# A routed expert stage with stationary weights, blocks of 448 tokens, and pad rows written during attention

## The chip, the cores and the metric

The kernel runs on one core of one Trainium2 chip. The metric is the device time of one execution in microseconds; the figure for the kernel before is the median of three runs. A difference of 0.3% (1.6 us) is about what such a measurement can tell from no change.

## The reference

Sixteen sequences of 100 tokens, 256 wide, go through a local cross-attention (16 heads, window 64) and then a feed-forward layer of eight experts with two experts per token. All in fp32. Cut to what matters here:

```
x = x + attention(layernorm(x), ctx)                 # 1600 tokens
xf = layernorm(x)
topk_p, topk_i = top_k(softmax(xf @ router_w.T), 2)
for e in range(8):
    mask   = (topk_i == e).any(-1)                   # tokens of expert e
    mean_w = mean of the normalised weights of those tokens
    h      = silu(xf @ gate_w[e].T) * (xf @ up_w[e].T)   # 256 -> 1024
    out   += mask * (h @ down_w[e].T) * mean_w           # 1024 -> 256
x = x + out
```

With the reference's own inputs the router gives the eight experts 374, 410, 299, 390, 438, 418, 425 and 446 tokens, 3200 in all. In tiles of 128 these are 3, 4, 3, 4, 4, 4, 4 and 4 tiles, 30 in all, as many as the trace has; in blocks of 448 they are one block each.

## The kernel before

**Attention stage.** Eight pairs of sequences go through a software pipeline written out in the code, one iteration of eight steps per pair. For each pair SP sends 16 small transfers (`kblk<-krot`, line 361) that spread the rotated keys over block-diagonal tiles; the scores (line 421) of the pair read them, so that SP's queue holds, in order, the key blocks of the next pair, then the store of the finished pair. Meanwhile the normalised rows and the row number of each token are scattered by POOL (line 1186) into a DRAM buffer `slots`, which has a region for each expert. ACT's queue loads the weights of expert 0 (`w_raw`, 3 MB) in iteration 1, and POOL splits them into a high and a low part.

**Between the stages.** DVE counts the tokens of each expert and makes a plan of tiles. POOL scatters a row of zeros behind the last token of each expert (`tailrow`, line 1223, eight scatters), so that the last tile of each expert is filled. SP waits for the scatters (line 385), reads the plan into registers, waits for the pad rows of the expert and loads a tile of 128 rows (`xin`, line 394).

**Expert stage.** Every fp32 product is made of three fp32r products: high x high, high x low, low x high. For a tile of 128 tokens TensorE keeps the tokens stationary: `x_hi` or `x_lo` (128 x 128) is loaded and 512 columns of the gate or up weights move (lines 615 to 617; 24 matmuls per tile, in two halves of the hidden width). The result has tokens on the partitions; ACT takes the silu, DVE multiplies (`h_sb`, line 1097), and TensorE transposes h in eight 128 x 128 pieces (line 631) into two banks, from which ACT makes `h_hi` (line 780) and DVE `h_lo` (line 1102). The down product (line 640) has h stationary and 256 columns of the down weights moving, 24 matmuls per tile. DVE copies the 128 x 256 result out (line 1109), POOL scales it by the mean weight (line 1245) and adds it to the output rows with an indirect transfer (line 1250).

**What sets the order.** Each engine has its own program, a loop over tiles inside a loop over experts; semaphores tie them. The gate and up of the next tile's first half (`hidden(next_par, 0)`) stand between the two halves of the down product, so that TensorE has work while h is prepared. The weights of the next expert are loaded a whole expert ahead into one of two buffers `w_raw`, and ACT (line 787) and DVE (line 1116) split them in 12 pieces of 512 columns, four in each of three tiles.

## Time and profile before

| | |
|---|---|
| three runs | 530.47, 531.59, 532.20 us; median 531.59 |
| span of the profiled execution | 528.9 us |
| TensorE matmuls busy | 476.4 us, 90% |
| TensorE weight loads busy | 375.3 us, 71% |
| DVE, ACT, POOL busy | 321.5, 265.6, 186.4 us |
| data moved | 46.26 MB, 87 GB/s in the mean |

The profiled execution is 2.7 us shorter than the median of the runs; sums below are made in its time and carried over by adding this. The page also has, for each of 40 slices of 13.2 us, the granted TensorE clock: full in nearly all, lower in slice 16 and 17, where the program passes from attention to the experts. The stages are: attention until about 200 us, routing and the first tile until 225 us, 30 tiles until 516 us, and a tail.

### The profile page before, as it was taken

The page shows a single profiled execution, that of the slowest core. Times are in us where ns is not written, and L with a number is a line of the kernel's source. Part 1 is how long each engine was busy: PE and PEld are TensorE (multiplying, and loading weights), DVE is VectorE, ACT ScalarE, POOL GpSimd, SP SyncE. Part 2 cuts the span into 40 slices and gives each one's busy share as a digit, 9 for nine tenths or more (in the row PEclk, how much of TensorE's full clock was granted, in tenths as well). Part 3 has the DMA queues.
Part 4 walks back from the last instruction along what each step waited for, and adds up shares of the span by engine and source line. Part 5 has one row for each costly group of instructions (what it writes and reads, how often), then busy time and mean ns, then how long its engine had stood idle before and what let it go on. Part 6 is the DMA issues. An engine that isn't in the chain of part 4 may idle for free. (4 is left out here: it accounts for less than half of the span.)

```text
span 528.9 us, 10721 instructions
## 1 busy us (share of the span) xinstructions
PE 476.4 (90%) x2879; PEld 375.3 (71%) x2880; DVE 321.5 (61%) x827; ACT 265.6 (50%) x878; POOL 186.4 (35%) x211
## 2 busy tenths in 40 slices
PE   2999999999999983199999999999999999999980
PEld 2656666665666542078888888888888888888870
DVE  3476988989998656345665456655655555553430
ACT  1287777677777870044544445544444444532320
POOL 5201327355372434712332323323333232232232
PEclk9699999999999995579999999999999999999996
DMA  7166102112020171371531634415317212112110
GB/s 210 33 184 241 32 12 54 32 34 63 7 58 14 50 286 47 96 274 32 168 117 35 215 83 139 147 32 196 101 20 256 42 20 32 27 21 39 20 20 10
DMA packets 21738, 46.26 MB, mean 87 GB/s; under 512 B 5032, under 2 KB 18600, under 8 KB 20684
## 3 DMA queue, kind: packets, MB, share of 16 engines
q10 hardware_dynamic: 1982, 23.29, 11.6%
q1 hardware_dynamic: 12974, 14.34, 9.3%
q0 software_dynamic: 6752, 8.29, 9.2%
q8 instruction: 11, 0.18, 0.1%
q14 instruction: 19, 0.16, 0.1%
HBM read 34.21 MB, written 10.04 MB: 84 GB/s over the span
## 5 line engine op out<-in xcount | busy, mean ns | idle before, releaser
L752 ACT ACTIVATE probs<-b_s,negmax 100x100 f32<-100x100 f32 x256 | 85.6, 358 | 25.2 <-DVE negmax L1005 21.8
L615 PE MATMUL b_s<-w_hi,x_hi 128*128 128x512 f32 x180 | 77.1, 428 | 1.1 <-issue 1.1
L617 PE MATMUL b_s<-w_hi,x_lo 128*128 128x512 f32 x180 | 72.3, 402 | 0.0
L616 PE MATMUL b_s<-w_lo,x_hi 128*128 128x512 f32 x180 | 72.2, 401 | 0.0
L640 PE MATMUL b_pv<-w_hi,h_hi 128*128 128x256 f32 x240 | 69.8, 291 | 1.4 <-DVE h_lo L1102 1.4
L640 PE MATMUL b_pv<-w_hi,h_lo 128*128 128x256 f32 x240 | 67.4, 281 | 0.0
L640 PE MATMUL b_pv<-w_lo,h_hi 128*128 128x256 f32 x240 | 67.3, 280 | 0.0
L1245 POOL TENSOR_SCALAR y_sb<-y_raw,mean 128x256 f32<-128x256 f32 x30 | 32.8, 1093 | 75.9 <-DVE y_raw L1109 75.7
L1250 POOL DMA_INDIRECT out<-y_sb,idnow x30 | 49.1, 1638 | 25.6 <-issue 23.0
L780 ACT CAST h_hi<-b_small 128x512 fp32r<-128x512 f32 x30 | 17.6, 587 | 80.7 <-PE b_small L631 80.7
L1116 DVE TENSOR_TENSOR w_lo<-w_raw,w_hi x84 | 57.3, 682 | 0.0
L752 ACT ACTIVATION_READ_ACCUMULATOR probs<-b_s,negmax 100x1 f32 x256 | 55.9, 218 | 0.0
L421 PE MATMUL b_s<-kblk,qrot 128*100 128x400 f32 x128 | 54.3, 505 | 0.0
L1102 DVE TENSOR_TENSOR h_lo<-b_small,h_hi 128x512 fp32r<-128x512 f32 x30 | 20.8, 692 | 55.0 <-ACT h_hi L780 55.0
L787 ACT CAST w_hi<-w_raw x84 | 52.2, 621 | 0.0
L776 ACT ACTIVATE act<-b_s 128x512 f32<-128x512 f32 x60 | 36.0, 600 | 28.6 <-PE b_s L617 28.6
L640 PEld LDWEIGHTS b_pv<-w_hi,h_hi 128*128 128x128 f32 x240 | 45.2, 188 | 3.0 <-DVE h_lo L1102 1.6
L640 PEld LDWEIGHTS b_pv<-w_lo,h_hi 128*128 128x128 f32 x240 | 45.3, 189 | 1.4
L640 PEld LDWEIGHTS b_pv<-w_hi,h_lo 128*128 128x128 f32 x240 | 45.2, 188 | 0.0
L1005 DVE TENSOR_REDUCE negmax<-b_s 100x4 f32<-100x400 f32 x64 | 36.2, 565 | 14.8 <-PE b_s L421 14.2
L1097 DVE TENSOR_TENSOR h_sb<-b_s,act 128x512 f32<-128x512 f32 x30 | 20.8, 692 | 34.7 <-PE b_s L617 34.7
L1176 POOL TENSOR_SCALAR ve<-mv 100x2 f32<-100x2 f32 x16 | 3.6, 228 | 103.8 <-DVE mv L859 103.8
(142 smaller groups left out, 1004.1 us busy)
## 6 DMA issues: line engine op xcount, KB each, us to landing
w_raw<-in_ffw ACTq DMA_DIRECT2D x7, 3072.0 KB, 10.1
xin<-slots SPq DMA_DIRECT2D x30, 128.5 KB
w_raw<-in_ffw SPq DMA_DIRECT2D x1, 3072.0 KB, 10.8
kblk<-krot SPq DMA_DIRECT2D x128, 12.5 KB, 1.8
out<-x_all SPq DMA_DIRECT2D x8, 200.0 KB
ctx_all<-in_ctxT SPq DMA_DIRECT2D x1, 1200.0 KB, 6.1
x_all<-in_x SPq DMA_DIRECT2D x1, 1200.0 KB
cst<-in_consts SPq DMA_DIRECT2D x1, 539.0 KB, 7.5
```

The source lines that it names most:

```text
L421: pe.matmul(o, qrot[:, i % 2, 2 * c + b, :], kblk[:, i % 2, c, h:h + QH, b * S:(b + 1) * S], start=False, stop=True).then_inc(s_s, 1)
L615: pe.matmul(o, lh, rh, start=(k == 0), stop=False)
L616: pe.matmul(o, lh, rl, start=False, stop=False)
L617: m = pe.matmul(o, ll, rh, start=False, stop=(k == n - 1))
L640: m = pe.matmul(b_y[:, 0:D], left[:, f, :], right[:, f, :], start=(f == 0 and k == 0), stop=(f == FC - 1 and k == 2))
L752: m = nc.scalar.activation(probs[:, N % 3, h, :], b_s[N % 3][0:S, h * S:(h + 1) * S], ACT.Exp, bias=negmax[:, N % 4, h:h + 1], accum_out=p ...
L776: nc.scalar.activation(act[:, half, :], b_gate[half][:, :], ACT.Silu).then_inc(s_act, 1)
L787: nc.scalar.copy(w_hi[1 - par][:, bass.ds(col, WC)], w_raw[par][:, bass.ds(col, WC)]).then_inc(s_whi, 1)
L1005: V.tensor_reduce(negmax[:, N % 4, :], b_s[N % 3][0:S, 0:QH * S].rearrange("p (h s) -> p h s", h=QH), AX.X, ALU.max, negate=True).then_inc ...
L1116: V.tensor_tensor(w_lo[1 - par][:, bass.ds(col, WC)], w_raw[par][:, bass.ds(col, WC)], w_hi[1 - par][:, bass.ds(col, WC)], ALU.subtract).t ...
L1245: G.tensor_scalar(y_sb[:, :], y_raw[:, :], mean1[:, 0:1], None, ALU.mult).then_inc(s_scaled, 1)
L1250: G.indirect_dma_start(out, bass.IndirectOffsetOnAxis(idnow[:, 0:1], 0), y_sb[:, :], None, bounds_check=TOK + P - 1, oob_is_err=True, comp ...
```

## The change

The expert stage is written anew, and the pad rows are written elsewhere.

- **Blocks.** A tile is now 448 tokens in four groups of 112 rows. `xin` is loaded as 112 partitions of four rows and transposed in 2 x 4 pieces of 112 columns into two banks.
- **Gate and up.** The weights are stationary (128 x 128) and 448 token columns move: 12 matmuls for each of eight strips f of 128 hidden features. The result has features on the partitions, which the down product wants, so h isn't transposed; `h_sb` is split by ACT and DVE from SBUF instead of PSUM.
- **Down.** For each strip and group, h (128 x 112) is stationary and 256 columns move, 12 matmuls per strip; the four groups' results lie in two banks. Strip f's down product stands behind the gate and up of strip f+2. The gate and up of the next block's strip 0 stand ahead of this block's last down strip.
- **Transpose of the next block** stands ahead of strip 7; its evacuation (`x_high` on ACT, `x_low` on DVE) can only begin when strip 7 has read the old `x_hi`.
- **Output.** ACT copies the two banks out with the mean weight as scale; POOL only issues four indirect transfers per block.
- **Weights.** One `w_raw` buffer, loaded, split and reloaded in six pieces of 1024 columns, one in each of strips 0 to 5 of an expert's first block.
- **Pad rows.** A host array `padrows` (448 rows of zeros with row numbers past the end) is copied by SP over the whole of `slots`, from DRAM to DRAM, in attention iterations 0 to 3: eight transfers of 461 KB in each, behind the key blocks of the next pair. POOL's scatter waits for those that cover its rows. The eight scatters of `tailrow` are gone, and so is SP's wait for them. The spare rows of the output are filled from `padrows` too (459 KB instead of 131 KB).

The diff, cut to its core:

```diff
-            sp.wait_ge(s_zero, 2)
-            sp.dma_start(out[TOK:TOK + P, :], tailrow[:, 0:D]).then_inc(s_pad, 16)
+            sp.dma_start(out[TOK:TOK + TILE, :], padrows[:, 0:D]).then_inc(s_pad, 16)
...
+            def fill_pads(j):
+                for e in range(E):
+                    base = e * REGION + j * TILE
+                    sp.dma_start(slots[base:base + TILE, :].rearrange("(p g) w -> p (g w)", g=GRP),
+                                 padrows.rearrange("(p g) w -> p (g w)", g=GRP)).then_inc(s_pre[j], 16)
...
             for i in pairs:
                 if i + 1 < NPAIR:
                     key_blocks(i + 1)
+                if i < MAXT:
+                    fill_pads(i)
                 if i >= 1:
                     store_x2(i - 1)
...
+            def hidden(par, f):
+                cols = slice(f * P, (f + 1) * P)
                 for which, banks, done in ((0, b_gate, s_gate), (1, b_up, s_up)):
                     wh, wl = wpart(w_hi[par])[which], wpart(w_lo[par])[which]
+                    o = banks[f % 2][:, 0:TILE]
+                    for c in range(DC):
+                        pe.matmul(o, wh[:, c, cols], x_hi[:, c, :], start=(c == 0), stop=False)
+                        pe.matmul(o, wh[:, c, cols], x_lo[:, c, :], start=False, stop=False)
+                        m = pe.matmul(o, wl[:, c, cols], x_hi[:, c, :], start=False, stop=(c == DC - 1))
...
-            def hidden_transpose(t, half):
-                pe.wait_ge(s_h, 2 * t + half + 1)
-                for f in range(HF):
-                    m = pe.transpose(b_ht[half][:, f * TILE:(f + 1) * TILE],
-                                     h_sb[:, half, f * P:(f + 1) * P], ident)
...
+            def step(t, par, next_par, next_split, following):
+                for f in range(1, FC):
+                    if f >= 2:
+                        pe.wait_ge(s_h, FC * t + f - 1)
+                    if f == FC - 1:
+                            pe.wait_ge(s_xlo, t + 1)
+                            tile_transpose(t + 1)
+                    hidden(par, f)
+                    if f >= 2:
+                        project_down(par, t, f - 2)
+                project_down(par, t, FC - 2)
+                    pe.wait_ge(s_wlo, next_split)
+                    pe.wait_ge(s_xlo, t + 2)
+                    hidden(next_par, 0)
+                project_down(par, t, FC - 1)
...
+            def take_output(t, e):
+                a.wait_ge(s_down, t + 1)
+                for n in range(GRP // 2):
+                    m = nc.scalar.activation(y_sb[:, 2 * n:2 * n + 2, :].rearrange("p g d -> p (g d)"),
+                                             b_y[n][0:ROWS, :], ACT.Copy, scale=meanw[0:ROWS, e:e + 1])
...
+                for n in range(GRP):
+                    G.indirect_dma_start(out, bass.IndirectOffsetOnAxis(idnow[:, n:n + 1], 0), y_sb[:, n, :], None,
```

How the order changes, at three places.

TensorE, from the last matmuls of a down half to the gate and up of the next tile, of the kernel before (`h_hi`, `h_lo` stationary; `x_hi` stationary; the wait `s_xlo` is for the next tile's tokens):

```order
L640 MATMUL b_pv<-w_lo,h_hi 128x256
L640 MATMUL b_pv<-w_hi,h_lo 128x256
L629 REGISTER_ALU
L631 MATMUL b_o<-cst,h_sb 128x128 [waits s_h]
L631 MATMUL b_o<-cst,h_sb 128x128 x3
L615 MATMUL b_s<-w_hi,x_hi 128x512 [waits s_xlo,s_wlo]
L616 MATMUL b_s<-w_lo,x_hi 128x512
L617 MATMUL b_s<-w_hi,x_lo 128x512
```

The same place of the kernel after, between two blocks:

```order
L628 MATMUL b_small<-w_lo,h_hi 112x256
L628 MATMUL b_small<-w_hi,h_lo 112x256
L615 MATMUL b_s<-x_hi,w_hi 128x448 [waits s_xlo,s_wlo]
L616 MATMUL b_s<-x_lo,w_hi 128x448
L617 MATMUL b_s<-x_hi,w_lo 128x448
```

The transposes of h are gone; the wait for the next tokens stands right behind a down strip, and what lies between strip 7's last gate and up matmul and this wait is two down strips, 24 matmuls.

SP's queue in the first iterations of attention, before (`kblk` are the key blocks of one pair, 16 transfers):

```order
L361 DMA kblk<-krot 16x200 [waits s_krot]
L361 DMA kblk<-krot 16x200 x15
L361 DMA kblk<-krot 16x200 [waits s_s,s_krot]
L361 DMA kblk<-krot 16x200 x15
L367 DMA out<-x_all 100x2x256 [waits s_x2]
```

and after:

```order
L345 DMA kblk<-krot 16x200 [waits s_krot]
L345 DMA kblk<-krot 16x200 x15
L357 DMA slots<-in_padrows 16x7196 x8
L345 DMA kblk<-krot 16x200 [waits s_s,s_krot]
L345 DMA kblk<-krot 16x200 x15
L357 DMA slots<-in_padrows 16x7196 x8
L351 DMA out<-x_all 100x2x256 [waits s_x2]
```

Eight copies of pad rows, of 16 pieces of 28.8 KB each, stand ahead of the key blocks of pair 2, and again ahead of those of pairs 3, 4 and 5.

ACT in a strip of an expert's first block, after:

```order
L771 ACTIVATE act<-b_s 128x448 [waits s_gate]
L775 CAST h_hi<-h_sb 128x448 [waits s_h]
L780 CAST w_hi<-w_raw 128x1024 [waits s_raw1_]
L784 DMA w_raw<-in_ffw 128x1024 [waits s_wlo]
L770 REGISTER_ALU
L771 ACTIVATE act<-b_s 128x448 [waits s_gate]
```

where before it had, in a tile with weight pieces:

```order
L780 CAST h_hi<-b_small 128x512 [waits s_ht]
L787 ISA
L787 COPY w_hi<-w_raw 128x512
L775 REGISTER_ALU
L776 ACTIVATE act<-b_s 128x512 [waits s_gate]
```

ACT now also waits, in each strip, for a piece of weights from DRAM and for DVE's split of the piece before.

## Rows read from the trace of the kernel before

**Rows 1.** The page, part 1: busy us (share of span) and instructions by engine.
```profile
PE 476.4 (90%) x2879; PEld 375.3 (71%) x2880; DVE 321.5 (61%) x827; ACT 265.6 (50%) x878; POOL 186.4 (35%) x211
```

**Rows 2.** Three stretches: us, busy us (xinstructions) by engine, granted clock, DMA.
```profile
core 0: us, PE busy (x) PEld busy (x) DVE busy (x) ACT busy (x) POOL busy (x), PEclk, DMA share, GB/s
0.00:218.00 218.00, 186.52 (x1139) 121.28 (x1140) 165.78 (x532) 138.57 (x643) 89.62 (x106) 0.94 0.27 84
218.00:231.00 13.00, 6.16 (x15) 4.18 (x15) 1.18 (x3) 2.25 (x3) 7.19 (x9) 0.51 0.45 128
231.00:516.00 285.00, 283.60 (x1726) 249.89 (x1726) 154.08 (x291) 124.83 (x232) 86.89 (x93) 1.00 0.33 92
```

**Rows 3.** Timeline of TensorE in one steady tile: start us, us, line, operation.
```profile
302.75 0.60 PE L631 MATMUL b_o<-cst,h_sb 128*128 128x128 f32 x4
303.10 0.48 PE L615 MATMUL b_s<-w_hi,x_hi 128*128 128x512 f32 x1
303.42 0.40 PE L616 MATMUL b_s<-w_lo,x_hi 128*128 128x512 f32 x1
303.66 0.39 PE L617 MATMUL b_s<-w_hi,x_lo 128*128 128x512 f32 x1
...
305.99 0.28 PE L640 MATMUL b_pv<-w_hi,h_hi 128*128 128x256 f32 x1
...
307.41 0.60 PE L631 MATMUL b_small<-cst,h_sb 128*128 128x128 f32 x4
```

**Rows 4.** Groups by shape, 250 to 500 us: busy us, mean ns | idle before.
```profile
L1116 DVE TENSOR_TENSOR w_lo<-w_raw,w_hi x76 | 51.8, 682 | 0.0
L787 ACT CAST w_hi<-w_raw x76 | 47.2, 621 | 0.0
L1102 DVE TENSOR_TENSOR h_lo<-b_small,h_hi 128x512 fp32r<-128x512 f32 x27 | 18.7, 692 | 49.3 <-ACT h_hi L780 49.3
L780 ACT CAST h_hi<-b_small 128x512 fp32r<-128x512 f32 x27 | 15.8, 587 | 71.9 <-PE b_small L631 71.9
L1087 DVE TENSOR_TENSOR x_lo<-b_proj,x_hi 128x256 fp32r<-128x256 f32 x26 | 10.9, 420 | 0.0
L772 ACT CAST x_hi<-b_proj 128x256 fp32r<-128x256 f32 x26 | 9.7, 374 | 16.8 <-PE b_proj L608 16.8
```

**Rows 5.** The one wait of SP on line 385, for the last scatter into slots.
```profile
L385 SPq EVENT_SEMAPHORE  x1: 28/28/28, 218.0 to 218.0; - x1
```

**Rows 6.** Timeline of all engines where the expert stage begins.
```profile
221.20 27.13 SPq L394 DMA_DIRECT2D xin<-slots  x4
222.91 0.66 PE L608 MATMUL b_proj<-cst,xin 128*128 128x128 f32 x2 [6.27 <-DMA xin<-slots]
223.66 0.37 ACT L772 CAST x_hi<-b_proj 128x256 fp32r<-128x256 f32 x1 [12.26 <-PE b_proj L608]
...
224.71 0.77 PE L615 MATMUL b_s<-w_hi,x_hi 128*128 128x512 f32 x1 [1.14 <-issue]
```

**Rows 7.** Timeline of all engines in the tail.
```profile
515.79 0.28 PE L640 MATMUL b_pv<-w_hi,h_lo 128*128 128x256 f32 x1
...
518.55 1.60 POOL L1250 DMA_INDIRECT out<-y_sb,idnow  x1 [0.84 <-issue]
```

**Rows 8.** The last wait of the program, on line 399, for the last added rows.
```profile
L399 SPq EVENT_SEMAPHORE  x1: 28/28/28, 522.5 to 522.5; - x1
```

**Rows 9.** Queues, 40 to 60 us, ACT queue: packets, MB, share of 16 engines.
```profile
q10 hardware_dynamic: 144, 3.15, 39.9%
```

**Rows 10.** Timelines of SP and PE: key blocks 2 and 3 sent, then read.
```profile
50.76 1.61 SPq L361 DMA_DIRECT2D kblk<-krot  x2
...
60.34 0.84 PE L421 MATMUL b_s<-kblk,qrot 128*100 128x400 f32 x2
...
71.75 10.31 SPq L361 DMA_DIRECT2D kblk<-krot  x16
...
82.79 0.84 PE L421 MATMUL b_s<-kblk,qrot 128*100 128x400 f32 x2
```

More of the change, by code:

```diff
@@ L61 @@
 C_BASE = C_EXP + E
[L62 to L63 removed]
+C_THR = C_BASE + E
 C_LT = C_THR + E * (MAXT - 1)
@@ L637, in project_down @@
+                    m.then_inc(done, 1)
+            def project_down(par, t, f):
+                pe.wait_ge(s_hlo, FC * t + f + 1)
+                if f == 0:
+                    pe.wait_ge(s_y, t + 1)
                 wh, wl = wpart(w_hi[par])[2], wpart(w_lo[par])[2]
-                for f in range(half * HF, (half + 1) * HF):
+                for g in range(GRP):
+                    o = b_y[g // 2][0:ROWS, g % 2 * D:(g % 2 + 1) * D]
                     for k, (left, right) in enumerate(((h_hi, wh), (h_hi, wl), (h_lo, wh))):
-                        m = pe.matmul(b_y[:, 0:D], left[:, f, :], right[:, f, :],
-                                      start=(f == 0 and k == 0), stop=(f == FC - 1 and k == 2))
@@ new lines, in step @@
+            def step(t, e, par, split, again, final=False):
+                for f in range(FC):
+                    if f:
+                        if f == FC - 1 and not final:
+                            a.wait_ge(s_up, FC * (t + 1))
+                            x_high(t + 1)
+                        silu(t, f)
+                    hidden_high(t, f)
+                    if split and f < WCH:
+                        weights_high(e, par, f)
+                    if split and again and 1 <= f <= WCH:
+                        reload(e, f - 1)
@@ new lines, in step @@
+            def step(t, e, par, split, final=False):
+                for f in range(FC):
+                    if f:
+                        if f == FC - 1 and not final:
+                            x_low(t + 1)
+                        gated(t, f)
+                    hidden_low(t, f)
+                    if split and f < WCH:
+                        weights_low(e, par, f)
+                    if f == FC - 2 and not final:
+                        v.wait_ge(s_idnow, t + 1)
+                        take_ids(t + 1)
```

396 lines of the change are left out of this document (151 added, 245 removed).

## The prediction, made before the changed kernel was run

> **What bounds the kernel now.** I read the busy time of the engines first: TensorE has matmuls in flight for 476.4 of 528.9 us [rows 1]. The table by stretch then says where: in the expert loop, 231 to 516 us, it is busy 283.6 of 285 us at the full clock, 2.4 GHz, while DVE, ACT and POOL are at half or less [rows 2]. So the stage is worth what TensorE's list of instructions costs, and nothing else. In attention (0 to 218 us) TensorE shows 186.5, DVE 165.8 and ACT 138.6 us: a chain through several engines. The change leaves its arithmetic alone, but puts 14.7 MB of copies under it. Between the stages TensorE runs at a mean granted clock of 0.51, that is at its lower level of 1.2 GHz, until 231 us [rows 2].
>
> **Gate, up and down.** The starts in one steady tile give the price of a matmul [rows 3]: from the second gate matmul (303.42) to the first down matmul (305.99) there are 11 of 512 columns, 0.2336 us each; from there to 307.41 are 12 of 256 columns, 0.1183 each. Both weight loads hide behind them. The line through the two gives 0.2048 us for 448 columns. A block has 96 of 448 and 96 of 256 columns: 19.66 + 11.36 = 31.02 us, eight blocks 248.2 us. The same work before was 30 tiles of 24 x 0.2336 + 24 x 0.1183 = 8.45 us, 253.4 us. So less padding (3584 rows instead of 3840) brings only 5 us; most is in what follows.
>
> **Transposes.** Before, each tile has two groups of four pieces of h. Four take 0.35 us (302.75 to 303.10), and the first matmul behind them is 0.32 instead of 0.234 us, so 0.435 a group, 0.87 us a tile, 26.1 us in 30 tiles; all of it goes. The transposes of x were two per tile and are eight per block: at 0.0875 each, with one transition of 0.085, 0.78 us a block, seven of them inside the loop, 5.5 us.
>
> **The seam between blocks.** `x_hi` has one buffer, so the next tokens can be evacuated only after strip 7's last gate and up matmul has started, at T. It shows 0.39 us [rows 3]; ACT starts 0.09 us after PE's end at stage entry (222.91 + 0.66 to 223.66) [rows 6]. ACT's casts cost 374 ns at 256 and 587 at 512 columns, DVE's subtractions 420 and 692 [rows 4]: at 448 columns 534 and 624, two of each now. The two hand-overs in this chain were 1.05 - 0.37 - 0.42 = 0.26 us (of the time from 223.66 to 224.71) [rows 4, 6]. Sum: T + 0.39 + 0.09 + 1.07 + 1.25 + 0.26 = T + 3.06. TensorE has two down strips to do meanwhile, until T + 0.205 + 24 x 0.1183 = T + 3.04. So the cover is just used up. I take 0.2 us for each of seven seams, 1.4 us, with bounds of 0 and 1 us each. Strip 7's own h (multiply, cast, subtract) is hidden by the 2.46 us of the next block's strip 0.
>
> **ACT and DVE per strip.** The weights are split in pieces of 1024 columns: at the same slopes a cast of 621 ns at 512 becomes 1.05 us, a subtraction of 682 ns 1.23 us [rows 4]. Cast of h, cast of weights, subtraction, next multiply form a ring: 0.57 + 1.05 + 1.23 + 0.62 + about 0.2 = 3.7 us, against TensorE's 2.46 + 1.42 = 3.88 per strip. It fits, and h has more than a strip of slack; two full 512-wide prices instead (1.24, 1.36) would make it 4.0 and cost some 0.1 x 6 x 7 = 5 us, less that slack. I take 0.
>
> **First hidden to last down matmul.** Before 515.79 - 224.71 = 291.1 us [rows 6, 7]. After 248.2 + 5.5 + 1.4 + the low clock. Before, it lasted about 6.3 us from the first matmul to 231 us [rows 2]; at half the rate this loses 3.1 us, and I take the same. Together 258.2: **-32.9 us**.
>
> **Stage entry.** The last scatter has landed at 218.0 [rows 5] and SP issues `xin` at 221.20 [rows 6]; in these 3.2 us SP loads two registers, now done ahead of the wait, and computes the address, still behind it. The gain lies between 0 and 3.2; I take half, -1.6. The load took 1.7 us for 131 KB; the 332 KB more cost 0.87 us at the rate below. Six more transposes at 1.2 GHz cost 6 x 0.175 = 1.05; x_high grows from 0.37 to 1.07, x_low from 0.42 to 1.25. Sum **+1.85 us**. The eight `tailrow` scatters on POOL lay beside all this and give nothing beyond the wait.
>
> **Tail.** Before, from the last matmul's start to the last indirect transfer's start 2.76 us, 3.95 to the end of the last wait, 6.4 to the end of the span [rows 7, 8]. After: 0.37, two ACT copies of 512 columns at 0.59 [rows 4], 0.84 until POOL starts [rows 7], then three more transfers at 1.60 and a gap of some 0.3 before the last: 8.1 us. **+5.3 us** (4 to 6, by how much 112 rows save on 128).
>
> **Pad rows during attention.** No row shows a copy from DRAM to DRAM. The nearest is the weight load: 3.15 MB took 39.9% of 16 engines over 20 us, 8.0 us of all of them, 394 GB/s [rows 9]; that is the upper end. A copy has DRAM at both its ends, and I take half, 197 GB/s, as the value, since nothing shows read and write sharing this path for free. A fill of eight copies is 3.69 MB: 9.4 or 18.7 us. The first goes out right behind key blocks 1, at about 40.5 us, and shares the engines with expert 0's weight load from 43.6. Key blocks 2 follow on the same queue from 50.8, and the scores want the first half at 60.3 [rows 10]. At full rate 3.69 + 3.15 MB are through by 59: no delay. At half rate, each engine taking a 28.8 KB piece in 2.3 us in turn with the load's 21.9 KB in 0.9, the fill is done at about 67 and the scores are 7 us late. I take **+6 us**, bounds 0 and 7.7. The later fills are alone: the second starts at about 62, is done by 82 to 87, and blocks 3 are wanted at 82.8 + 6 [rows 10]: just covered, and so the next two. The issues themselves (8 per fill) lie in SP's idle time, 62 to 71.75. POOL waits for the fills only an iteration or more later. The 459 KB copy at the start meets a DMA that is busy with the first loads: +0 to 1.5, I take **+0.5**.
>
> The Trainium skill gives a measured rate for this. "DMA: Bandwidth & Descriptors", section "Latency and other measured facts", has copies between two DRAM tensors at 207 to 214 GB/s in each direction. By it a fill takes 17.2 us and the first delay is about 5 us instead of 6; no run of before shows it.
>
> **Sum.** 528.9 - 32.9 + 1.85 + 5.3 + 6 + 0.5 = 509.65 us; the profiled execution is 2.66 below the median, so **512.3 us**.
>
> **Rivals.**
> 1. *The fills cost nothing.* If DRAM to DRAM runs near 394 GB/s, the 6 us go: 506.3. For: the DMA engines' share is only 0.27 in attention [rows 2]. Against: every byte goes through DRAM twice.
> 2. *Seams cost more.* At each block's end ACT must be free at T, SP's tokens there, and TensorE's program jumps over a loop body three times as long as before, behind 12 queued down matmuls that cover 1.42 us. If the chain or a fetch of code costs 0.6 to 1.9 us at each of eight seams, that is 5 to 15 us: 517 to 527. Against: before, the loops of 30 tiles jump as often and only 1.4 of 285 us are without matmul [rows 2]. The Trainium skill, "Runtime: NRT & Kernel Launch", section "Instruction fetch mechanics", says a taken branch to a place outside the pages at hand stalls until the target is fetched; no row of before shows such a stall in this loop.
> 3. *Slower than before.* The fills run so slowly that all four hold back the key blocks of the pair behind them. Between the start of a fill and the need of those blocks lie some 20 us. At rate r a fill takes 3690/r us (r in GB/s) and each of the last three costs what exceeds 20, the first 8 more. The loss reaches the 25 us that decide at a fill of about 24 us, 150 GB/s; at 120 GB/s a fill takes 31 us, 3 x 11 + 19 = 52 us: 558. Against: that is under two fifths of what the weight load shows [rows 9].
> 4. *More gained.* Fills free and entry, tail and low clock at their lower ends: 500 to 503.5.
>
> **Chances.** Forecast (509 to 516) 0.42; fills free, 505 to 508, 0.24; dearer seams, 517 to 527, 0.15; slow fills 0.11, of which 0.08 end slower than before; more gained 0.08. The likeliest gives 512.3. The range takes in the first two and half of the third: 503.5 to 522. Faster by over 0.3% (which is about what a measurement can tell from no change) 0.88, within 0.3% 0.03, slower 0.09.
>
> **What would show it.** Gate and up matmuls 0.205 us apart, down 0.118; a block 31.8 us; no idle TensorE inside a block; at a seam 0 to 0.4 us before `b_s<-x_hi`, behind DVE's `x_lo`. The scores of pair 2 near 66 instead of 60.3 us, waiting for `kblk`, and the later pairs still 22.4 us apart (82.79 - 60.34). First gate matmul near 233 us (226.6 without the fill's delay), last down matmul near 491, 18.5 us of tail. What would make it wrong: a copy rate far from 200 GB/s, a router that gives one expert over 448 tokens on the chip (one more block, +32 us; the largest has 446), or a strip period above 3.9 us.

## The result and the profile after

The changed kernel takes 551.26 us (median of four runs, 549.86 to 552.11), the kernel before 531.04 beside it: a ratio of 1.0376, 95% interval 1.0353 to 1.0399. It is slower by 3.8%, where 512.3 us was forecast, with a range up to 522.

The page of the changed kernel (busy time; the span in 40 slices of 13.8 us, TensorE first; the granted clock; the queue that carries instructions; the costliest group of TensorE):

```profile
span 550.2 us, 8828 instructions
...
PE 453.4 (82%) x2739; PEld 370.0 (67%) x2740; DVE 305.4 (56%) x719; ACT 265.3 (48%) x845; POOL 137.0 (25%) x130
PE   2799799989898994069999579999399995899970
...
PEclk9899899999999996569999879999699998799995
...
q8 instruction: 43, 0.70, 0.5%
...
L615 PE MATMUL b_s<-x_hi,w_hi 128*128 128x448 f32 x192 | 74.2, 386 | 30.2 <-issue 27.7
```

TensorE's busy time fell by 23.0 us against [rows 1], as it should with less padding and no transposes of h, and yet the span grew by 21.3. Three holes stand in TensorE's row inside the expert stage (the 57, the 3, the 58), each with a dip of the clock in the same slices. TensorE's idle time there, from the waits after the first tile (us in total, times, longest):

```profile
PE b_s L615 <- issue: 25.9, 3, 8.9
PE b_pt L615 <- issue: 2.5, 4, 1.0
```

"Issue" means that the profile shows no semaphore or transfer that ended the idle time; the label alone doesn't prove that there was none, which is what the experiments are for. This is the first of the three on TensorE's timeline (start, duration, instruction; in brackets the idle time before it):

```profile
309.17 0.28 PE L628 MATMUL b_o<-w_hi,h_hi 128*112 128x256 f32 x1
...
310.47 0.28 PE L628 MATMUL b_small<-w_hi,h_lo 128*112 128x256 f32 x1
319.66 0.74 PE L615 MATMUL b_s<-x_hi,w_hi 128*128 128x448 f32 x1 [8.91 <-issue]
320.20 0.58 PE L616 MATMUL b_s<-x_lo,w_hi 128*128 128x448 f32 x1
...
323.56 0.50 PE L616 MATMUL b_pt<-x_lo,w_hi 128*128 128x448 f32 x1
```

The last down matmul of a block is followed by nothing for 8.91 us, and then the matmuls start 0.37 us apart (1.2 GHz) until about 323.9, from where they are 0.205 apart. The others are at 394.51 (8.46 us) and 469.52 (8.52 us). They lie 75 us apart, which is two blocks: exactly where TensorE's loop over pairs of experts jumps back. Right behind that jump the program has a second one, forward over the loop body for further blocks of the pair's first expert, which no expert needs; a stop is the price of both. The four short ones (280.59, 355.87, 430.82 and 506.51; 0.35 to 1.0 us) lie behind the other forward jump, that of the pair's second expert: not at the jump, but each time at the tenth matmul of the block. One more stop, 1.82 us at 244.24, lies in the first block, at its forward jump.

The span against the forecast's sum, all in the time of the profiled execution. The marks are the last scatter seen by SyncE (229.2), the first gate matmul (237.92), the last down matmul (533.16) and the end (550.2), against 218.0, 224.71, 515.79 and 528.9 before [rows 5 to 7].

| stretch (us) | before | forecast | after |
|---|---|---|---|
| start to last scatter | 218.0 | 224.5 | 229.2 |
| to first gate matmul | 6.7 | 8.6 | 8.7 |
| to last down matmul | 291.1 | 258.2 | 295.2 |
| to the end | 13.1 | 18.4 | 17.0 |

So two terms failed: the expert stage, by 37.0 us, and attention, by 4.7.

### The profile page after: what moved, and what is told of

Same layout as the page of the kernel before. It is cut to its first block, busy times and chain, and to the rows that moved or that the text cites. A ratio compares the mean times of both kernels' runs of the same rounds, so it can differ in the third digit from the quotient of the medians.

```text
span 550.2 us, 8828 instructions
## 1 busy us (share of the span) xinstructions
PE 453.4 (82%) x2739; PEld 370.0 (67%) x2740; DVE 305.4 (56%) x719; ACT 265.3 (48%) x845; POOL 137.0 (25%) x130
## 3 DMA queue, kind: packets, MB, share of 16 engines
q10 hardware_dynamic: 6302, 23.29, 13.8%
## 4 chain that ended last, share of the span: by engine, by line
PE 63%; DVE 12%; issue 11%; ACT 4%; DMA 3%; POOL 3%; SPq 2%; ACTq 0%; DVEq 0%; POOLq 0%
PE b_small L628 8%; PE b_o L628 8%; PE b_s L615 8%; PE b_s L616 7%; PE b_s L617 7%; PE b_s L416 4%; PE b_pt L615 3%; PE b_pt L616 3%; PE b_pt L617 3%; ACT probs L745 2%; PE b_proj L470 2%; DVE xn L866 2%; PE b_pv L439 2%; DVE negmax L1000 2%; PE b_pt L425 2%
## 5 line engine op out<-in xcount | busy, mean ns | idle before, releaser
L615 PE MATMUL b_s<-x_hi,w_hi 128*128 128x448 f32 x192 | 74.2, 386 | 30.2 <-issue 27.7
L775 ACT CAST h_hi<-h_sb 128x448 fp32r<-128x448 f32 x64 | 36.3, 567 | 82.6 <-DVE h_sb L1089 81.5
L616 PE MATMUL b_s<-x_lo,w_hi 128*128 128x448 f32 x192 | 72.8, 379 | 0.0
L617 PE MATMUL b_s<-x_hi,w_lo 128*128 128x448 f32 x192 | 72.5, 378 | 0.0
L1093 DVE TENSOR_TENSOR h_lo<-h_sb,h_hi 128x448 fp32r<-128x448 f32 x64 | 40.1, 626 | 55.6 <-ACT h_hi L775 55.6
L615 PEld LDWEIGHTS b_s<-x_hi,w_hi 128*128 128x128 f32 x192 | 37.6, 196 | 34.2 <-issue 31.5
L1098 DVE TENSOR_TENSOR w_lo<-w_raw,w_hi 128x1024 fp32r<-128x1024 f32 x42 | 51.5, 1226 | 13.7 <-ACT w_hi L780 13.7
L780 ACT CAST w_hi<-w_raw 128x1024 fp32r<-128x1024 f32 x42 | 44.0, 1047 | 0.0
L617 PEld LDWEIGHTS b_s<-x_hi,w_lo 128*128 128x128 f32 x192 | 37.5, 196 | 3.5
L616 PEld LDWEIGHTS b_s<-x_lo,w_hi 128*128 128x128 f32 x192 | 37.8, 197 | 2.5
## 6 DMA issues: line engine op xcount, KB each, us to landing
kblk<-krot SPq DMA_DIRECT2D x128, 12.5 KB, 1.8
```

The lines of the kernel that those rows point to most:

```text
L615: pe.matmul(o, wh[:, c, cols], x_hi[:, c, :], start=(c == 0), stop=False)
L616: pe.matmul(o, wh[:, c, cols], x_lo[:, c, :], start=False, stop=False)
L617: m = pe.matmul(o, wl[:, c, cols], x_hi[:, c, :], start=False, stop=(c == DC - 1))
L780: nc.scalar.copy(w_hi[1 - par][:, cols], w_raw[:, cols]).then_inc(s_whi, 1)
L1093: V.tensor_tensor(h_lo[:, f, :], h_sb[:, f % 2, :], h_hi[:, f, :], ALU.subtract).then_inc(s_hlo, 1)
L1098: V.tensor_tensor(w_lo[1 - par][:, cols], w_raw[:, cols], w_hi[1 - par][:, cols], ALU.subtract).then_inc(s_wlo, 1)
```

## The experiments

Each is timed beside the kernel before, on the same chip (530.6 to 531.4 us in all of them).

### The three stops: TensorE's code

**e2_straight.** TensorE's eight blocks in straight code; the loops for further blocks are left out (with these inputs they are never entered).

```
-            with pe.Fori(0, E // 2) as ep:
-                for par in range(2):
-                    ...
-                    with pe.If(end - lo), pe.Fori(lo, end) as t:
-                        step(t, par, par, split, None)
-                    step(end, par, 1 - par, split_next, following)
+            for e in range(E):
+                step(e, e % 2, ...)
```

> The changed kernel with TensorE's expert part written out eight times in a row, without the loop over pairs of experts and without the loop for experts that need more than one block (that loop is left out; with these inputs no expert needs it). Theory (code fetch at the jump back): the three idle stretches of 8.9, 8.5 and 8.5 us at 319.7, 394.5 and 469.5, which end by 'issue' and not by a semaphore, are the refetch of TensorE's code when the loop over pairs jumps back; with straight code they go (25.9 us), so do the low-clock matmuls behind each (about twelve at 0.37 instead of 0.205, 2.0 us each, 6 us) and the short ones at the jumps over the inner loop bodies (0.8, 0.4, 0.4, 1.0): 33 to 35 us less, 516 to 519. Rival (the pause is TensorE waiting for something of another engine that the records do not show, such as the output additions or the weights): the stretches stay at the same places, 551. Second rival (code is fetched too slowly in straight code too, as a loop's first round shows none of it but at 244.2 with 1.8 us): eight steps with a stall of 1 to 2 us each, 525 to 533.

Measured: 514.14 us, 37.1 less than the changed kernel and 3.1% faster than before (ratio 0.9689, 0.9672 to 0.9706). No idle time by "issue" is left after the first gate matmul. The theory holds, with some 2 us more than expected: 516 to 519 was. It doesn't tell yet whether any jump back costs this, or only a long one.

**e5_loop2.** The loop over pairs stays, the two inner loops for further blocks go, which are left out of the computation (with these inputs they are never entered).

```
-                    with pe.If(end - lo), pe.Fori(lo, end) as t:
-                        step(t, par, par, split, None)
-
                     step(end, par, 1 - par, split_next, following)
```

> The changed kernel with TensorE's loop over pairs of experts kept, with its register work, but the inner loops for further blocks left out, so that the loop body is two block steps long instead of four. Theory A (the length of code that the jump spans decides): the body is about half as long, near that of the kernel before, whose jumps back show 1.1 us at most; the three stretches of 8.5 to 8.9 us shrink to about 1 us and the time is 518 to 525. Theory B (each jump back costs the same, whatever lies in the body, since the engine has to begin its fetch anew): three stretches of 8.5 us stay and only the jumps over the inner bodies (0.4 to 1.0 each) go: 548 to 550. Rival (the registers that are read at the start of a pair): as B, the stretches stay.

Measured: 513.09 us (0.9672, 0.9654 to 0.9690), and no stop. That is 5 us below Theory A's range, which left 1 us at each jump. The loop jumps back as often and reads the same registers, so Theory B and the registers are out: what decides lies in the inner loops that are gone, and they are never entered. Their mere number isn't it: e10_compact_only below has two inner loops in the body and no stop. What is left is how much code the body holds.

**e8_loop3.** The inner loop goes for one expert of the pair only: three block steps in the body.

```
-                    with pe.If(end - lo), pe.Fori(lo, end) as t:
-                        step(t, par, par, split, None)
+                    if par == 1:
+                        with pe.If(end - lo), pe.Fori(lo, end) as t:
+                            step(t, par, par, split, None)
```

> The changed kernel with the loop for further blocks left out for the first expert of each pair only, so that the body of TensorE's loop over pairs is three block steps long (four in the changed kernel, where each jump back stopped TensorE for 8.5 to 8.9 us; two in the version without inner loops, where no stop is seen). Theory A (a bound between two and four steps: code that fits is at hand, code that doesn't is fetched anew from memory at each jump): either no stop as with two steps, 513 to 516 with the one kind of forward jump, or the whole stop of 8 to 9 us at each of three jumps, 545 to 549. Theory B (the stop grows with the distance jumped): three stops of about 4 us, 526 to 532.

Measured: 516.3 us (0.9739, 0.9680 to 0.9798), the four runs from 514.5 to 520.6, so at the upper edge of Theory A's first case; the spread is wider than in the other versions, and nothing here explains it. TensorE's waits after the first tile, and the instruction queue of this kernel's page:

```profile
PE b_s L615 <- issue: 2.2, 1, 2.2
```
```profile
q8 instruction: 14, 0.23, 0.2%
```

One stop, of 2.25 us, at 277.46, where the forward jump passes a body that has not been fetched yet; in the later rounds neither that jump nor the jump back stops anything. So there is a bound between three and four block steps, and Theory B (in proportion to the distance, 526 to 532) is out.

The packets give the scale. These are the instruction packets of e2_straight, of e5_loop2, and of the changed kernel from 309 to 384 us, one round of its loop:

```profile
q8 instruction: 22, 0.36, 0.3%
```
```profile
q8 instruction: 13, 0.21, 0.2%
```
```profile
q8 instruction: 9, 0.15, 0.8%
```

A packet is 0.70 MB / 43 = 16.3 KB. The straight version and e5_loop2 differ by six block steps, 1180 matmuls in the program, so 9 x 16.3 KB / 1180 = 124 bytes for a matmul with its weight load (an estimate: one packet more or less makes it 110 or 138). A block step has 192 matmuls and 8 transposes, 25 KB: the body is 100 KB in the changed kernel, 75 KB with three steps, 50 KB with two, and 29 KB in the kernel before (four steps of 58). From 309 on the changed kernel brings in nine packets in each of its three rounds, 147 KB, so more than its whole body anew. In e8_loop3 the last packet comes at 292 us: from 293 to 515 us its view has no instruction packet at all, and a body of 75 KB jumps back three times from what is at hand.

**e4_unroll.** Eight experts written out, the loop for further blocks kept in each: no jump back over a long body, but forward jumps over code that is met for the first time.

```
+            for e in range(E):
+                par = e % 2
+                lo, hi, end, following = tiles_of(pe, e)
+                with pe.If(end - lo), pe.Fori(lo, end) as t:
+                    step(t, par, par, WCH * (e + 1), None)
+                step(end, par, 1 - par, WCH * (e + 2), None if e < E - 1 else False)
```

> The changed kernel with TensorE's loop over pairs of experts written out for the eight experts, the loop for further blocks of an expert kept in each (so that nothing is left out), which leaves no jump back over a long body but eight jumps forward over a loop body of one block each. Theory (only the jump back over a body of four block steps is dear): as the straight version, 514.1, plus eight forward jumps at the 0.35 to 1.0 us that they showed in the changed kernel (0.6 in the mean, some 5 us): 517 to 521. Rival (skipping a body costs as much as the trace showed only because the body was already at hand from the round before; in code that is met for the first time each forward jump has to fetch anew): eight times 2 to 4 us, 530 to 546.

Measured: 531.09 us, as long as before (1.0003, 0.9977 to 1.0029). My theory fell and the rival holds, at its lower end. TensorE's waits after the first tile:

```profile
PE b_s L615 <- issue: 12.6, 6, 2.5
```

The stage from first gate to last down matmul is 273.1 us against 256.8 in the straight version. I had taken the price of a forward jump from the short stops of the changed kernel. Here, where each jump passes code that is met for the first time, it is 2.1 to 2.5 us in five cases, 1.0 in one (the first), and nothing at two (the second and the fifth expert); why those two go free, no run shows. The 16.3 us that the stage is longer are these 12.6 and, behind two of them, matmuls 0.37 us apart at the lower clock. Writing a program out is no cure by itself when what is written out must be jumped over.

**e9_oneadd.** Is the stop long because GpSimd's output additions use the same transfer engines? Three of the four additions per block are left out.

```
-                for n in range(GRP):
+                for n in range(1):
                     G.indirect_dma_start(out, ...
```

> The changed kernel with one of the four output additions of each block kept and three left out (so three of four rows of each block are missing from the output). It asks why one jump back takes 8.5 to 8.9 us: in the changed kernel TensorE's instruction packets of 16 KB move one at a time about 3.5 us apart there, while GpSimd's four indirect transfers of the block before run on the same transfer engines from 315 to 322. Theory (the fetch is slow by itself: so many packets one after another): the three stops stay 8.5 to 8.9 us; only the tail after the last matmul is shorter, by three additions at 1.77 us, 5.3 us: 545 to 547. Rival (the additions' traffic or GpSimd's descriptor writing holds the instruction packets up): the stops shrink to 3 to 6 us each, and the time is 530 to 538.

Measured: 543.39 us, 7.9 less and 1.6 below the theory's range. Of this 7.3 is the tail, 9.7 us from the last down matmul to the end instead of 17.0 (I had counted 5.3). The stops stay: 8.82, 8.67 and 8.41 us. So the additions are not what makes them long. What does is seen only in part. The transfers of the changed kernel from 306 to 322 us:

```profile
q0 software_dynamic: 512, 0.46, 25.2%
q8 instruction: 4, 0.07, 1.7%
```

Four instruction packets; in steps of half a microsecond the view has them at 309, 313, 316.5 and 320 us, one at a time; in e4_unroll two lie around a forward stop (308 and 311.5). Some 3.5 us for each packet and three in a row would give the nine us. Why TensorE goes on after three of them here, and after one at a forward jump, no run here shows. The stop holds two jumps, one back and one forward; by the prices of e4_unroll the forward one would be about a quarter of it (an estimate).

### Attention: GpSimd's pieces and the first fill

In the changed kernel the rotary step of the keys came at these times (VectorE's timeline; pairs 2 to 5 of 0 to 7):

```profile
49.86 0.58 DVE L878 TENSOR_TENSOR krot<-proj,swap 128x400 f32<-128x400 f32 x1
...
76.37 0.57 DVE L878 TENSOR_TENSOR krot<-proj,swap 128x400 f32<-128x400 f32 x1
...
100.78 0.57 DVE L878 TENSOR_TENSOR krot<-proj,swap 128x400 f32<-128x400 f32 x1
...
125.17 0.57 DVE L878 TENSOR_TENSOR krot<-proj,swap 128x400 f32<-128x400 f32 x1
```

Before, they were at 50.15, 71.14, 94.07 and 116.94: from pair 2 to pair 3 it is 26.5 instead of 21.0 us, and from there on 24.4 instead of 22.9, though the fills end after four iterations. The lengthening that goes on was in no term of the forecast. Its place, on the changed kernel's timeline:

```profile
139.86 1.03 POOL L1186 CAST w_hi<-w_raw 128x1024 fp32r<-128x1024 f32 x1
...
139.92 3.54 DVE L866 TENSOR_SCALAR xn<-x_all,mv,rstd 100x256 f32<-100x256 f32 x2 [0.70 <-POOL rstd L1153]
...
140.97 2.35 POOL L1189 TENSOR_TENSOR w_lo<-w_raw,w_hi 128x1024 fp32r<-128x1024 f32 x1
```

VectorE's two small steps take 1.12 us beside GpSimd's cast (1.03) and 2.50 beside its subtraction (2.35), and end with it (143.46 and 143.32); where GpSimd is idle the two take 0.73 together. With pieces of 1024 columns instead of 512 they end 1.5 us later.

**e1_pool512.** GpSimd's pieces back to 512 columns.

```
-                    cols = slice((i - 1) * WC, i * WC)
-                    G.tensor_copy(w_hi[0][:, cols], w_raw[:, cols])...
+                    for half in range(2):
+                        cols = slice((i - 1) * WC + half * WC // 2, (i - 1) * WC + (half + 1) * WC // 2)
+                        G.tensor_copy(w_hi[0][:, cols], w_raw[:, cols])...
```

> The changed kernel, with one edit: GpSimd splits the first expert's weights during attention in pieces of 512 columns again (two to an iteration) instead of one of 1024. Theory (piece width): in the changed kernel an attention iteration takes 24.4 us (rotary steps of the keys from 100.8 to 125.2 to 149.6) against 22.9 before, and VectorE's xn<-x_all steps that lie beside GpSimd's 1024-wide split take 3.5 us each against 2.0 beside the 512-wide one; with 512-wide pieces the period goes back to 22.9, so six to seven iterations give back 1.5 us each: 9 to 10 us less than the changed kernel, some 541 to 542. Rival (the transfers that fill the padding rows, or the wider hidden-layer buffers, lengthen the iterations): the period stays 24.4 and the time 551. Second rival (GpSimd's total work, not its piece, delays the key blocks): the work is the same or somewhat more here, so again 551 or later.

Measured: 546.15 us, 5.1 less. The same place and two rotary steps in this kernel:

```profile
137.96 0.60 POOL L1187 CAST w_hi<-w_raw 128x512 fp32r<-128x512 f32 x1
...
138.02 2.04 DVE L866 TENSOR_SCALAR xn<-x_all,mv,rstd 100x256 f32<-100x256 f32 x2 [0.70 <-POOL rstd L1153]
...
138.64 1.27 POOL L1190 TENSOR_TENSOR w_lo<-w_raw,w_hi 128x512 fp32r<-128x512 f32 x1
```
```profile
77.47 0.57 DVE L878 TENSOR_TENSOR krot<-proj,swap 128x400 f32<-128x400 f32 x1
...
100.39 0.57 DVE L878 TENSOR_TENSOR krot<-proj,swap 128x400 f32<-128x400 f32 x1
```

The mechanism is right, the period is 22.9 us again; the size is half of what I wrote. Only four whole periods follow (6.0 us), and the iteration that holds the first fill ends 1.1 later, not earlier: there the fill is what is waited for, whatever GpSimd does.

**e12_before1024.** The same cause, the wide piece, put alone into the kernel before.

```
-                    for n in range((i - 1) * WCH // 6, i * WCH // 6):
-                        cols = slice(n * WC, (n + 1) * WC)
+                    for n in range((i - 1) * WCH // 12, i * WCH // 12):
+                        cols = slice(2 * n * WC, 2 * (n + 1) * WC)
```

> The kernel before with one edit: GpSimd splits the first expert's weights in one piece of 1024 columns per attention iteration instead of two of 512. It adds one suspected cause to the kernel that lacks all the rest of the change (no fills, other expert stage). Theory (the piece width alone makes VectorE's steps beside it 3.5 us long and each such iteration 24.4 instead of 22.9 us): the last rotary step of the keys moves from 162.7 to 169 to 172, and the time from 530.6 to 537 to 540. Rival (the width acts only together with the fills or with the changed order of semaphores): the period stays 22.9 and the time within 1 us of 530.6.

Measured: 538.76 against 531.12 us (1.0149, 1.0121 to 1.0177): 7.6 us for the width of one instruction pair. The last rotary step is at 171.69 instead of 162.72, 9.0 us later, of which some 1.3 don't reach the end, and `xn` takes as long as in the changed kernel:

```profile
162.00 3.60 DVE L871 TENSOR_SCALAR xn<-x_all,mv,rstd 100x256 f32<-100x256 f32 x2 [0.71 <-POOL rstd L1179]
...
163.10 2.35 POOL L1213 TENSOR_TENSOR w_lo<-w_raw,w_hi 128x1024 fp32r<-128x1024 f32 x1
```

The Trainium skill ("SBUF — State Buffer", section "SBUF: two separate sides") says that VectorE, in some forms of its instructions, and GpSimd share a pair of ports which the first comer holds for a whole instruction. The traces agree: each of the two steps starts within 0.1 us of an instruction of GpSimd and lasts 0.1 to 0.2 us longer than it, whether it takes 0.60 and 1.27 us (narrow pieces) or 1.03 and 2.35 (wide ones).

**e3_late_fill.** Each fill one iteration later.

```
-                if i < MAXT:
-                    fill_pads(i)
+                if 1 <= i <= MAXT:
+                    fill_pads(i - 1)
```

> The changed kernel with each of the four transfers that fill padding rows issued one attention iteration later (in iterations 1 to 4 instead of 0 to 3), so that the first no longer competes with the first load of the expert weights and lies behind the issue of the second block of keys. Theory (the first fill delays the third and later key blocks): krot of the third pair came 5.2 us later than before, 1.5 of them the longer period, 3.7 the first fill; this kernel is 3 to 4 us faster than the changed one, 547 to 548. Rival (any fill costs the same wherever it is issued, since the bandwidth or SyncE's issue of eight transfers, 5.2 us, is taken from the loads of keys in each iteration): same time, 551. Third possibility (the period of 24.4 is due to the fills): the iterations without a fill would be shorter, and only the place of the long ones moves; 551 too, but visible in the periods.

Measured: 546.98 us, 4.3 less. The load of expert 0's weights lands after 10.0 us; in the changed kernel it shared the engines with the fill (issues of its page: engine, count, KB each, us to landing), and TensorE stood still once before the scores:

```profile
slots<-in_padrows SPq DMA_DIRECT2D x32, 449.8 KB, 8.1
...
w_raw<-in_ffw ACTq DMA_DIRECT2D x1, 3072.0 KB, 18.8
```
```profile
63.72 0.34 PE L414 MATMUL b_s<-mask_bf,ident_bf 100*100 100x400 bf16 x1 [3.81 <-issue]
```

The profile says "issue" here too, though the program waits at this place for key blocks. Those issued from 50 to 60 us took 9.0 us to land in the changed kernel and 2.1 in the kernel before (the rows of the two, in this order):

```profile
kblk<-krot SPq DMA_DIRECT2D x14, 12.5 KB, 9.0
```
```profile
kblk<-krot SPq DMA_DIRECT2D x13, 12.5 KB, 2.1
```

With the fill later they take 2.3, and the scores start at 60.06 instead of 63.90. Pair 3's rotary step comes at 72.35 instead of 76.37. The periods behind it stay 24.4; that the later fills hold up nothing is seen in e11_compact below, which has all four and the narrow pieces, and whose periods are 22.9 (71.23, 94.12, 117.00), as before.

### All of it together

**e6_all** is e4_unroll with the edits of e1 and e3; **e7_straight_all** is e2_straight with them.

> The changed kernel with three edits, nothing left out: TensorE's eight experts written out with the loops for further blocks kept, GpSimd's split of the first expert's weights in pieces of 512 columns, and the four fills one iteration later. Theory (three separate causes, which add up): the last rotary step of the keys moves from 173.9 to about 163.5, where the kernel before has it (162.7), so 9 to 10 us less than the version with only the experts written out (which I expect at 517 to 521): 508 to 511. Rival (the two edits in attention remove the same delay twice: each alone gave 5.1 and 4.3 us, and the later fills now meet the later key loads): 512 to 516.

Measured: 520.75 us (0.9815, 0.9782 to 0.9848). The absolute forecast missed, since it stood on e4_unroll's 517 to 521; the step that it was to measure, 10.3 us from e4_unroll, is as expected, and the last rotary step (163.08) too.

> The version with eight experts in straight code (the loop for further blocks of an expert is left out), with the two edits in attention (splits in pieces of 512 columns, fills one iteration later). It has no jump at all in TensorE's expert part, so it gives the time of the blocks themselves. Theory (causes add up): 514.1 less the 10.3 us between the two unrolled versions: 503 to 505. Rival (straight code met for the first time hides small stops): it ends above the version with the short loop body by over 1.5 us.

Measured: 502.38 us (0.9465, 0.9441 to 0.9488), 0.6 below the expectation and as fast as the short loop body below, so the rival, small stops in straight code, is out.

**e10_compact_only** and **e11_compact** leave nothing out. TensorE's body is one block step per expert, run once per block; only the first strip of the next block (12 gate and up matmuls, not the 24 that an expectation names) is written twice, under two conditions. The body has 424 matmuls, 53 KB. e11_compact has the two edits in attention as well.

```
                 project_down(par, t, FC - 2)
+                with pe.If(end - t):
+                    pe.wait_ge(s_xlo, t + 2)
+                    hidden(par, 0)
+                with pe.If((end - t - 1) & 64), pe.If(following):
+                    pe.wait_ge(s_wlo, pe.to_reg(WCH * (e + 2)))
+                    pe.wait_ge(s_xlo, t + 2)
+                    hidden(1 - par, 0)
                 project_down(par, t, FC - 1)
...
-                    with pe.If(end - lo), pe.Fori(lo, end) as t:
-                        step(t, par, par, split, None)
-                    step(end, par, 1 - par, split_next, following)
+                    with pe.Fori(lo, hi) as t:
+                        step(t, e, par, end, following)
```

> The changed kernel with the shorter loop body on TensorE alone (one block step for each expert of a pair, run once per block, the next block's first hidden part written twice under two conditions), nothing left out and attention as in the changed kernel. It closes the account: changed kernel 551.3, this one, and the one with the two edits in attention added, 502.5. Theory (the costs add up; the attention edits gave 10.3 us between the two unrolled versions): 502.5 + 10.3 = 512.8, so 511.5 to 514. Rival (the two sets of edits interact, for instance because a later entry into the expert stage meets another state of TensorE's clock or of its code): 508 or less, or 516 or more.

Measured: 514.2 us (0.9679, 0.9649 to 0.9710), 0.2 above the expectation, and no stop by "issue".

> A candidate that leaves nothing out: the changed kernel with (1) a shorter loop body on TensorE: one block step for each expert of a pair, run once for each block of that expert, with only the first hidden part of the next block written twice under two conditions (body some 2.3 block steps long instead of four), (2) GpSimd's split in pieces of 512 columns, (3) the fills one iteration later. Theory (code of up to three block steps stays at hand, so neither the jump back nor the short jumps over 24 matmuls have to fetch; the attention edits give the 10.3 us that they gave between the two unrolled versions, 531.1 and 520.8): the version with two steps took 513.1, less 10.3, plus up to 0.4 for each of eight skipped parts: 503 to 506. Rival (every jump forward, and the loop's own end, costs 1 to 2 us, as in the version written out, where each jump over one block step stopped TensorE for 2.1 us in the mean): 8 to 16 us more, 511 to 519.

Measured: **502.45 us** (501.99 to 503.36 in five runs) against 531.12: 0.9466, 0.9445 to 0.9487; 503 to 506 was expected. That is 5.3% faster than before, 8.9% faster than the change as made, and as fast as straight code. Its page, and its expert stage in the table by stretch (length, PE, PEld, DVE, ACT and POOL busy with their counts, clock, DMA share, GB/s):

```profile
span 500.6 us, 8895 instructions
...
PE 445.5 (89%) x2739; PEld 364.9 (73%) x2740; DVE 302.6 (60%) x719; ACT 263.3 (53%) x845; POOL 139.3 (28%) x142
...
PEclk9999999999999999557999999999999999999995
...
q8 instruction: 13, 0.21, 0.2%
```
```profile
231.00:484.00 253.00, 252.82 (x1583) 238.46 (x1581) 135.72 (x191) 121.10 (x198) 45.53 (x35) 1.00 0.40 99
```

TensorE is busy 252.8 of 253 us at the full clock; this is the stage that the forecast described.

## Why the prediction was wrong

- **Gate, up and down: right.** The matmuls of 448 columns start 0.205 us apart (0.2048 interpolated), those of 256 columns 0.12. The stage without stops is 483.55 - 227.03 = 256.5 us in e11_compact, against 258.2; the low clock at its start costs 2.5 us there, against 3.1.
- **Transposes: right.** Eight of x cost 0.70 us up to the next gate matmul, whose successor starts 0.29 later instead of 0.205: 0.78.
- **The seam as a chain of ACT and VectorE: right in kind, free in fact.** No gate matmul waits for `x_lo` after the first tile; the 1.4 us were not paid.
- **The jump: this step failed.** It stands in rival 2, as a fetch of code of "0.6 to 1.9 us at each of eight seams", set aside because the loops before "jump as often and only 1.4 of 285 us are without matmul" [rows 2]. That row speaks of a body of 29 KB, and no jump of the kernel before shows a stop there: TensorE's waits are one for `h_lo` (1.4 us) and one for `h_sb` (0.8). The change makes it 100 KB, and the rival said so (a loop body three times as long), but priced it as if a longer body meant a somewhat longer pause. It is a bound that is crossed: 8.5 to 8.9 us at three places, 25.9 us, plus some 12 matmuls at the lower clock behind each, which start 0.37 instead of 0.205 us apart (3 x 2.0 = 6 us), plus 2.5 us in the four short stops and 1.8 at the first forward jump, with nine such matmuls behind it (1.5): 37.7 us in all, of the 38.4 by which the stage is longer than in e2_straight. e2, e5, e8 and e10 show the cause and its size: without the long body the time falls by 35.0 to 38.2 us. The sentence that the rival quoted from the Trainium skill ("Runtime: NRT & Kernel Launch", section "Instruction fetch mechanics": a taken branch out of the two pages at hand stalls until its target is fetched) has the right kind of cost and the wrong bound. By two pages of 16 KB the jumps back over 50 and 75 KB would have stopped as well; they show no stop and bring in no packet. The same section gives TensorE 128 KiB for instructions, and a body of 100 KB would fit if all of that served a loop; here it doesn't stay, and 75 KB does. The measurement decides.
- **ACT and VectorE per strip: right.** 1.05 and 1.23 us for pieces of 1024 columns were the estimates, 1.047 and 1.226 the means; strips follow each other at 3.885 us (3.88).
- **GpSimd's pieces of 1024 columns: left out.** The forecast widened the pieces for ACT and VectorE and never asked who else uses the width `WC`. This term was put at nothing without a reason. Alone in the kernel before it costs 7.6 us. The sign of it was in the trace of before: `xn` took 2.04 us beside GpSimd's cast and subtraction, and 0.73 where GpSimd was idle.
- **First fill: the wait is right, the rate was mis-sized, and the size comes near by luck.** Forecast 6, bounds 0 and 7.7. It lengthens that iteration by 4.0 us beside the wide pieces (26.5 against 22.5 in e3_late_fill) and by 6.2 beside the narrow ones (77.47 against 71.23 for pair 3 in e1_pool512 and e11_compact): the two delays lie partly over each other. But the copies don't run at 197 GB/s. From 62 to 77 us, with the second fill nearly alone, and from 40 to 60, with the first fill beside the weight load, the queues of the changed kernel were (q1 has the fills, q10 the weights):

```profile
q1 hardware_dynamic: 530, 3.92, 76.4%
```
```profile
q1 hardware_dynamic: 457, 3.77, 51.2%
q10 hardware_dynamic: 136, 3.10, 41.9%
```

  3.92 MB (a fill and 0.24 MB beside it) in 76.4% of 15 us is 342 GB/s by the same working that gave the forecast its 394, above both its 197 and the 207 to 214 that it quotes from the Trainium skill. The fill and all but 0.05 MB of the weights had moved by 60 us, which is nearly the forecast's case of full rate, "no delay"; the delay came all the same, since the key blocks took 9.0 us to land while both were under way. So two steps failed against each other, the rate and "through by 59: no delay". The later fills are covered, as forecast. The 0.5 us for the copy at the start isn't seen: the last rotary step is at 162.74 in e11_compact and at 162.72 before.
- **Entry and tail: near, with terms that offset each other.** At the entry +2.0 against +1.85: `xin` goes out 1.0 us behind the last scatter (230.19) instead of 3.2, where 1.6 was taken off, but its load takes 3.5 us, not 2.6. From the last down matmul to the start of the last indirect transfer it is 540.91 - 533.16 = 7.75 us against 8.1 (the forecast's terms make 7.5 with one gap of 0.3, as it is written, and 8.1 with three), and the tail as a whole is 1.4 shorter than forecast.

The account: 550.2 - 509.65 = 40.6 us, of which 37.0 are in the expert stage, 4.7 before the last scatter (the pieces, less the oversized fill), 0.2 at the entry and -1.4 in the tail.

## What to carry to other kernels

Count the code of a loop body, entered or not, before writing a body larger: bodies up to 75 KB jumped back at no cost on TensorE, one of 100 KB cost some 10.6 us at every jump back (stop and low clock), and a row from a shorter loop says nothing on it. A branch that is never taken is not free either; fold rare cases into one body rather than writing the body twice, or writing the program out. When a constant sets the width of an instruction, look up each engine that uses it: GpSimd's width was paid by VectorE.

## What the runs showed of the hardware

- A loop body of 75 KB stays at hand from round to round (no instruction packet in e8_loop3 from 293 to 515 us); one of 100 KB is brought in anew in each round (nine packets of 16.3 KB in the changed kernel).
- A jump forward over 25 KB of code that was never fetched stops TensorE for 2.1 to 2.5 us in six cases of ten (five in e4_unroll, one in e8_loop3), for 1.0 and 1.8 us in two (the first of e4_unroll and of the changed kernel), and not at all in two (e4_unroll). Where the loop stays at hand, in the later rounds of e8_loop3, it stops nothing.
- A stop costs more than its length when the granted clock falls behind it: after 8.91 us (319.66) matmuls start 0.37 apart for 4.2 us, after 2.25 us in e8_loop3 (277.46) for 3.2 us, and after 2.26 us in e4_unroll (310.91) for some 3 us, but after 2.52 us in the same kernel (347.10) they are 0.205 apart at once. The rows don't show why one of the short stops has it and another has not.
- In the changed kernel the core moved 382 GB/s between 50 and 60 us with a fill and a weight load under way together, and transfers of 12.5 KB then took 9.0 us to land instead of 2.1. A copy from DRAM to DRAM in pieces of 28.8 KB moved 342 GB/s in the time that it kept the engines busy.
- GpSimd's cast and its subtraction each hold back a small step of VectorE for their whole length: two steps on 100 x 256 elements took 0.73 us alone, 2.04 beside pieces of 512 columns and 3.54 beside 1024.
